# A GRU scan with an expert feed-forward beside it: first x copies ahead of the start state, sixteen early input shares, and GpSimd's weight splitting in smaller pieces over more steps

## What is computed

```python
def cell(h, x):                              # 32 steps, one after the other
    gi = x @ W_ih + b_ih                     # [32, 256] @ [256, 768]
    gh = h @ W_hh + b_hh
    r = sigmoid(i_r + h_r); z = sigmoid(i_z + h_z)
    n = tanh(i_n + r * h_n)
    return (1.0 - z) * n + z * h
# xt: the 1024 states
probs = softmax(xt @ w_router)               # 128 experts, top 4
basis = silu(xt @ w_gate) * (xt @ w_up)      # 8 bases of 128
out   = (mix of the bases by the 4 experts' coefficients) @ w_down
out  += (silu(xt @ shared_w_gate) * (xt @ shared_w_up)) @ shared_w_down
return x + out
```

## Time and profile before

| | us |
|---|---|
| median of 3 runs | 152.83 |
| lowest and highest | 152.21, 153.01 |
| the profiled execution | 153.46 |
| its span in the profile | 151.7 |

### The profile page before, as it was taken

The page is one execution under the profiler, slowest core; times in us unless marked ns, Lnnn a source line. Parts: engine busy times, 40 slices in busy tenths (PEclk is TensorE's granted clock), DMA queues, the critical chain, the costliest instruction groups (busy, mean ns, idle before and its releaser), DMA issues.

```text
span 151.7 us, 4005 instructions
## 1 busy us (share of the span) xinstructions
PE 137.6 (91%) x1480; PEld 97.8 (64%) x1480; DVE 110.7 (73%) x407; ACT 69.2 (46%) x224; POOL 63.6 (42%) x115
## 2 busy tenths in 40 slices
PE   7559798689798979999999999999999999899991
PEld 4236575457465557766776687667766777588881
DVE  2020868789979988898879777977797779858661
ACT  1200757865458246526633553256334542613730
POOL 1200515566315771474138314741465145657030
PEclk9955999999999999999999999999999999999999
DMA  2999980000000000010000000000010001000102
GB/s 79 312 371 210 288 278 5 4 4 0 0 0 4 0 0 4 2 35 6 0 16 23 0 0 12 29 0 6 2 36 0 0 4 37 0 0 0 35 4 69
DMA packets 5619, 7.12 MB, mean 47 GB/s; under 512 B 864, under 2 KB 4192, under 8 KB 5600
## 3 DMA queue, kind: packets, MB, share of 16 engines
q1 hardware_dynamic: 5180, 6.63, 15.2%
q10 hardware_dynamic: 420, 0.24, 0.6%
HBM read 5.81 MB, written 1.05 MB: 45 GB/s over the span
## 4 chain that ended last, share of the span: by engine, by line
PE 67%; DVE 19%; DMA 5%; ACT 4%; issue 2%; ACTq 1%; DVEq 0%
PE unit L609 29%; PE gates L600 14%; PE gates L561 8%; PE down L674 6%; DMA h<-in_cond_dram 5%; DVE sc_out L842 4%; DVE sc_add L836 2%; DVE keys L925 2%; PE unit L576 2%; DVE pre L833 2%; DVE hT L849 2%; ACT sc_add L416 2%; DVE m L830 1%; PE route L621 1%; PE route L655 1%
## 5 line engine op out<-in xcount | busy, mean ns | idle before, releaser
L306 POOL CAST hThi<-hT 128x64 fp32r<-128x64 f32 x32 | 8.2, 255 | 64.9 <-DVE hT L849 64.4
L609 PE MATMUL unit<-whi,hThi 128*128 128x512 f32 x80 | 33.8, 423 | 1.2 <-DVE shared L902 0.9
L409 ACT ACTIVATE trz<-gates 128x128 f32<-128x128 f32 x32 | 8.9, 277 | 53.2 <-PE gates L600 53.2
L600 PE MATMUL gates<-whh,hT 128*32 128x192 f32 x512 | 28.1, 338 | 4.6 <-DVE hT L849 4.5
L609 PE MATMUL unit<-whi,hTlo 128*128 128x512 f32 x80 | 31.6, 395 | 0.0
L609 PE MATMUL unit<-wlo,hThi 128*128 128x512 f32 x80 | 31.6, 395 | 0.0
L600 PEld LDWEIGHTS gates<-whh,hT 128*32 128x32 f32 x512 | 13.7, 111 | 16.1 <-DVE hT L849 8.7
L842 DVE TENSOR_TENSOR_SCAN sc_out<-sc_mul,sc_add 128x128 f32<-128x128 f32 x32 | 15.7, 492 | 7.2 <-ACT sc_add L416 7.0
L609 PEld LDWEIGHTS unit<-whi,hThi 128*128 128x128 f32 x80 | 15.1, 188 | 6.7 <-issue 2.7
L561 PE MATMUL gates<-wih,xT 128*32 128x192 f32 x320 | 17.8, 346 | 1.3 <-DVE xT L808 1.3
L609 PEld LDWEIGHTS unit<-whi,hTlo 128*128 128x128 f32 x80 | 15.0, 188 | 3.6
(11 more groups left out here) (126 smaller groups left out, 232.3 us busy)
## 6 DMA issues: line engine op xcount, KB each, us to landing
wraw<-in_L_ffn_w_gate_dram SPq DMA_DIRECT2D x2, 512.0 KB, 9.0
wraw<-in_L_ffn_w_up_dram SPq DMA_DIRECT2D x2, 512.0 KB, 11.2
out_dram<-ot SPq DMA_DIRECT2D x7, 128.0 KB
wih<-in_L_cond_W_ih_dram SPq DMA_DIRECT2D x1, 768.0 KB, 6.0
xtok<-in_x_dram SPq DMA_DIRECT2D x4, 192.0 KB, 9.3
whh<-in_L_cond_W_hh_dram SPq DMA_DIRECT2D x1, 512.0 KB, 7.2
whh<-in_L_cond_W_hh_dram SPq DMA_DIRECT2D x1, 256.0 KB, 6.1
wraw<-L_ffn_shared_w_gate_dram SPq DMA_DIRECT2D x1, 256.0 KB, 11.4
```

Source lines behind the costliest of these rows:

```text
L600: last = pe.matmul(g[Q * j:Q * (j + 1), HN:HN + 3 * FJ], st, whh[:, s, :].rearrange("p (g j c) -> p j g c", g=3, j=NJ)[:, j], start=False, ...
L609: last = pe.matmul(dst, st[:, p % 3, s, :, :].rearrange("p t b -> p (t b)"), w[:, s, :, cols], start=(s == 0 and n == 0), stop=(s == KB - ...
```

## The change

- **Start.** VectorE's two copies of the first x chunks stand ahead of its wait for the start state. W_ih comes in two transfers, one for each half of the contraction. TensorE's warming matmuls are 16, 0 and 3 in place of 13, 2 and 2. The rest of x is loaded ahead of the router's and the gate weights.
- **Early shares.** Sixteen steps in place of twelve have their input share made early, two of each chunk, all by step 5. All of x is transposed by step 3 instead of step 5; two of the three pairs are copied by VectorE instead of ScalarE.
- **Splitting.** The router's high part is made in step 1 instead of 0, its low part in step 2 instead of 0. The high parts stand in steps 2 to 6 instead of 0 to 6, the low parts in steps 3 to 8 instead of 0 to 6. GpSimd takes seven pieces instead of six, each as two instructions of 128x256; `lo_down` is three instructions of 128x256 and stands in step 10 instead of 9.

```diff
-WARM = 13
+WARM = 16
-EARLY = [4, 5, 6, 7, 8, 9, 12, 13, 10, 14, 16, 17]
-EARLY_PAIRS = [[0], [1], [2], [3], [4], [5]]
-TURN_PAIR = {1: 2, 3: 4, 5: 6}
-KEEP_PAIR = {1: 2, 3: 4, 5: 6}
-HI_AT = [(0, 1), (1, 2), (2, 4), (4, 5), (5, 7), (7, 9), (9, 10)]
-LO_VECTOR_AT = [[], [1], [3], [], [5], [7], []]
-LO_POOL_AT = [[0], [], [2], [4], [6], [8], [9]]
+EARLY = [4, 5, 6, 7, 10, 11, 14, 15, 18, 19, 22, 23, 26, 27, 30, 31]
+EARLY_PAIRS = [[0], [1], [2], [3, 4], [5], [6, 7]]
+TURN_PAIR = {1: 2, 2: 4, 3: 6}
+KEEP_PAIR_SCALAR = {1: 2}
+KEEP_PAIR_VECTOR = {2: 4, 3: 6}
+HI_AT = [(0, 0), (0, 0), (0, 2), (2, 4), (4, 6), (6, 8), (8, 10)]
+LO_VECTOR_AT = [[], [], [], [], [], [3], [5], [7]]
+LO_POOL_AT = [[], [], [], [0], [1], [2], [4], [6], [8, 9]]
...
             load_x(sp, range(0, 2), 0, 2, ld_xfirst)
-            sp.dma_start(wih[:, :, :], pairs(w_ih)).then_inc(ld_wih, 16)
+            for s in range(KB):
+                sp.dma_start(wih[:, s, :], pairs(w_ih)[:, s, :]).then_inc(ld_wih, 16)
...
+            load_x(sp, range(TC), 2, NC, ld_xrest)
             sp.dma_start(rraw[:, :, :], pairs(w_router)).then_inc(ld_router, 16)
...
-                if pair == 0:
-                    load_x(sp, range(TC), 2, NC, ld_xrest)
...
                 pool.wait_ge(w_hi, i + 2)
-                pool.tensor_tensor(wlo[:, s, :, cols], wraw[:, s, :, cols], whi[:, s, :, cols].bitcast(F32),
-                                   ALU.subtract).then_inc(w_lo_pool, 1)
+                for a in range(2):
+                    last = pool.tensor_tensor(wlo[:, s, a, cols], wraw[:, s, a, cols], whi[:, s, a, cols].bitcast(F32),
+                                              ALU.subtract)
+                last.then_inc(w_lo_pool, 1)
...
-                    if t == 2 * TC + 1:
+                    if t == TC + SKEW + 4:
                         lo_down()
...
-                if t == 0:
+                if t == 1:
                     hi_router()
...
-                        pe.wait_ge(x_pair_turned, 3)
+                        pe.wait_ge(x_turned, 4)
...
-            keep_warm(2)
             turn_x(0, route, 0)
             turn_x(1, unit_bank[2], 0)
-            keep_warm(2)
+            keep_warm(3)
...
+            keep_x(0)
+            keep_x(1)
             dve.wait_ge(ld_h0, 16)
             dve.transpose(hT0[:, :].rearrange("p (s b) -> p s b", s=KB), h0[:, :].rearrange("p (c s) -> p s c", s=KB)).then_inc(hT_ready, 1)
             dve.tensor_scalar(hhalf[:, :], h0[:, :], 0.5, None, ALU.mult).then_inc(hhalf_ready, 1)
-            keep_x(0)
-            keep_x(1)
...
+                if t in KEEP_PAIR_VECTOR:
+                    keep_x_pair(KEEP_PAIR_VECTOR[t])
-                if t == 0:
+                if t == 2:
                     lo_router()
```

More of the change, by code:

```diff
@@ L147, in build @@
         early_bank = unit_bank + [turned, down]
-        pair_bank = {2: route, 4: route, 6: route}
         scaled_up = qc[:, 0:2 * UW].rearrange("p (n c) -> p n c", n=2)
@@ L339, in lo_piece @@
                 pool.wait_ge(w_hi, i + 2)
-                pool.tensor_tensor(wlo[:, s, :, cols], wraw[:, s, :, cols], whi[:, s, :, cols].bitcast(F32),
-                                   ALU.subtract).then_inc(w_lo_pool, 1)
+                for a in range(2):
+                    last = pool.tensor_tensor(wlo[:, s, a, cols], wraw[:, s, a, cols], whi[:, s, a, cols].bitcast(F32),
+                                              ALU.subtract)
+                last.then_inc(w_lo_pool, 1)
             def lo_down():
                 pool.wait_ge(w_hi, len(PIECES) + 2)
-                pool.tensor_tensor(dlo_w[:, :, :], draw[:, :, :], dhi_w[:, :, :].bitcast(F32), ALU.subtract)\
-                    .then_inc(w_lo_pool, 1)
+                for a in range(3):
+                    last = pool.tensor_tensor(dlo_w[:, a, :], draw[:, a, :], dhi_w[:, a, :].bitcast(F32), ALU.subtract)
+                last.then_inc(w_lo_pool, 1)
             def mixing(f):
@@ L402, in keep_x_pair @@
                 act.wait_ge(x_raised, c + 2)
-                act.activation(xT[:, c:c + 2, :, :].rearrange("p c s n -> p (c s n)"), pair_bank[c][:, 0:4 * P],
-                               ACT.Copy)\
+                act.activation(xT[:, c:c + 2, :, :].rearrange("p c s n -> p (c s n)"), route[:, 0:4 * P], ACT.Copy)\
                     .then_inc(x_pair_turned, 1)
@@ L474, in prepare @@
                     load_gates(t + 2)
-                if t == 0:
+                if t == 1:
                     hi_router()
-                if t in KEEP_PAIR:
-                    keep_x_pair(KEEP_PAIR[t])
+                if t in KEEP_PAIR_SCALAR:
+                    keep_x_pair(KEEP_PAIR_SCALAR[t])
                 if t < len(HI_AT):
@@ L543, in wait_x @@
             def wait_x(t):
-                if t // TC < 2:
-                    pe.wait_ge(x_turned, t // TC + 1)
+                c = t // TC
+                if c < 2:
+                    pe.wait_ge(x_turned, c + 1)
+                elif c < 4:
+                    pe.wait_ge(x_pair_turned, 1)
                 else:
-                    pe.wait_ge(x_pair_turned, t // TC // 2)
+                    pe.wait_ge(x_turned, c // 2 + 1)
             def x_part(t):
@@ L557, in x_part @@
                 if t == 0:
-                    pe.wait_ge(ld_wih, 16)
+                    pe.wait_ge(ld_wih, 32)
                 for s in range(KB):
@@ L581, in turn_x_pair @@
             def turn_x_pair(c):
-                if c > 2:
-                    pe.wait_ge(x_pair_turned, c // 2 - 1)
-                else:
-                    pe.wait_ge(x_turned, 2)
-                turn_x(c, pair_bank[c], 0)
-                turn_x(c + 1, pair_bank[c], 1)
+                wait_x(TC * (c - 1))
+                turn_x(c, route, 0)
+                turn_x(c + 1, route, 1)
             def h_part(t):
@@ L809, in keep_x, with keep_x_pair @@
                     .then_inc(x_turned, 1)
+            def keep_x_pair(c):
+                dve.wait_ge(x_raised, c + 2)
+                dve.tensor_copy(xT[:, c:c + 2, :, :].rearrange("p c s n -> p (c s n)"), route[:, 0:4 * P])\
+                    .then_inc(x_turned, 1)
             def keep_early(n):
```

## The result

The changed kernel takes 152.65 us (median of 20 runs, 150.72 to 154.25) against 152.88 for the kernel before (20 runs, 151.71 to 153.59). The ratio to before is 0.9931, 95% interval 0.9905 to 0.9956.

What follows compares the result with a forecast made beforehand. Bounds: the start, then the recurrence's latency, then TensorE's work in the long stretch. Terms -1.95 + 4.05 - 0.25 - 3.6 = -1.75 us, from the profiled 153.46 to 151.7, hence a median of 151.0; range 148.4 to 153.4.

Steps and rivals of the forecast that it cites:

- H(1): Start of `h_part` (H) of step 1: predicted to move from 16.80 to 14.85 us, a gain of 1.95.
- x lands as before: Start: x's transfers stay first in both queues, so transposes still start at 7.81 us.
- Still early enough: Start: the last part of W_hh, with one more issue ahead, lands by 10.5 us at most, ahead of need.
- Step 8: Early steps: unit 3 waits for GpSimd's piece 6, with VectorE's piece 7 getting between; 4.5 us with the coefficients.
- Step 9: Early steps: unit 4 needs GpSimd's pieces 8 and 9, the latter there at 3.6 us; the step takes 4.4.
- the second half of the unit follows: Step 9: after GpSimd's piece 9, only half of unit 4 remains, 0.8 us.
- The long stretch: Steps 18 to 29: fewer just-in-time input shares, 14.4 us per four steps instead of 15.58; a gain of 3.6.
- Pieces covered: Rival, steps 8, 9 and 12: waits for GpSimd fall away, up to 2.65 us less, 148.4 us; chance 0.24.
- No earlier clock: Rival, start: TensorE's clock rises no earlier than before, costing 1.0 us, 152.0 us; chance 0.14.
- VectorE the bound: Rival, long stretch: VectorE falls behind TensorE; each 0.4 us per four steps costs 1.2, up to 153.4 or 154.6; chance 0.14.
- Halving turns against it: Rival, steps 6 to 11: VectorE gets in at ten new boundaries, delaying GpSimd's pieces; 3.3 us more, 154.3; chance 0.10.
- The wait for `em`: Near the end: TensorE's wait for VectorE grows from 0.35 to 1.0 us, using up step 30's 0.65; nothing gained.

Runs made afterwards that it cites:

- again: The changed kernel run once more, unchanged, for a second trace: median 152.43 us, ratio 0.9928 to the kernel before.
- spread_down11: Changed kernel with low-part pieces placed a step earlier, VectorE taking the last, and `lo_down` in step 11 instead of 10: 149.0 us, ratio 0.9753.
- d11_balance: `spread_down11` with VectorE's pieces 1, 3, 5, 7 in steps 3 to 6 and GpSimd's six in steps 2 to 7: 147.99 us, ratio 0.9657.
- warm9: Changed kernel plus twenty warming matmuls on TensorE in step 9, ahead of unit 4: 151.28 us, ratio 0.9884.
- d11_early12: `spread_down11` with the old twelve early shares, one pair in each of steps 0 to 5: 152.48 us, ratio 0.9969.
- spread_whole: Changed kernel with low-part pieces placed a step earlier, VectorE taking the last, and GpSimd's pieces as one instruction each: 150.88 us, ratio 0.9886.

## Why the prediction was right, and what it missed

The sum was made against the profiled execution, 151.7 us for its like. It took 151.24. That the profile fell into the lower heap is luck: the trace of `again`, with the same code, took 152.92. The forecast for the median, 151.0, missed the measured 152.65 mostly by what the sum did not have in it, the fall of the clock behind step 9. Term by term:

| term | predicted | measured in the profile |
|---|---|---|
| H(1) | 16.80 to 14.85: -1.95 | 14.57: -2.2 |
| steps 1 to 12 | 46.1: +4.05 | 45.9: +3.9 |
| steps 13 to 17 | 17.85: -0.25 | 17.8: -0.3 |
| steps 18 to 29 | 3 x 14.4: -3.6 | 3 x 14.35: -3.65 |
| from step 30 on | 0 | -0.05 |

**The start came out in sum, not by its steps.** "x lands as before" was wrong: it was used at 6.12, 1.7 earlier. "Still early enough" for W_hh was wrong: its last part was issued 0.5 later, as predicted, but landed 7.8 us after its issue and not 7.2, at 11.1, and with everything else earlier it is what opens step 0. The clock did not rise at 11.7; it had been at 1.0 since before 6 and fell there. That H(1) is so near is two errors against each other. A path much like the one that I described is that of other executions: `spread_down11` has the shares at 8.99 (predicted 9.5), H(0) at 11.55 (11.9) and H(1) at 15.00 (14.85).

**Steps 1 to 7** were 3.69, 3.41, 4.06, 2.92, 3.28, 3.62, 4.09 for 3.41, 3.41, 4.06, 2.95, 3.4, 3.7, 4.5. The first is longer by the clock, which is low until 15.1 (in `again`, with the clock back before H(1), it is 3.40). The last is 0.4 shorter than the sum had it, for a piece of 0.68 us ahead of the quarter k0; why was not traced.

**Step 8** was 4.42 for 4.5, and TensorE's wait named `wlo`, 0.78 us. But `spread_down11`, with no piece outstanding there, has the same 4.42: there TensorE waits 0.54 us for VectorE's `q`, and the coefficients close both steps 4.13 us after H(8). So GpSimd's piece had no price of its own; only `d11_balance`, where VectorE has no piece in step 7 either, gets 3.35. Right size, wrong wait.

**Step 9** was 4.89 for 4.4. The step that failed is "the second half of the unit follows": both waits stand ahead of the unit's first matmul, so unit 4 begins only when the second piece is there, at 47.39, and all six matmuls (48.95 - 47.39 = 1.6 us) come after it, not three. The piece itself was 0.3 earlier than in the sum (47.39 - 44.06 = 3.3 for 3.6). What I had not in the sum at all is the second cost of such a wait: in three of the four traces with a wait of 2.47 us TensorE ran at 1.2 GHz for some 3 us afterwards, a loss of 1.4 to 1.7 us over steps 9 to 12; by the times (11 of 20 in the upper heap) it may be about half of the executions. Filling the wait (`warm9`) brings the median from 152.65 to 151.28. I had looked for the clock at the start and not in the middle, though the terms of my sum had the wait in them.

**Step 12** was 4.23 for 4.25, with the wait for `mixed`; `spread_down11` confirms its cause.

**The long stretch.** 14.35 for 14.4, and `d11_early12` gives the 3.6 us back: the right term with the right cause. VectorE did not become the bound by more than the 0.1 of the forecast, and the tie was real:

```profile
80.89 0.25 DVE L855 STREAM_TRANSPOSE hT<-sc_out 128x64 f32<-128x64 f32 x1
81.14 0.41 DVE L921 TENSOR_REDUCE lx<-route 128x128 f32<-128x256 f32 x1
...
85.34 0.25 DVE L855 STREAM_TRANSPOSE hT<-sc_out 128x64 f32<-128x64 f32 x1
```

The state after the quarter k0 is there at 85.59, H(20) is 85.64 and 7.37 us after H(18) = 78.27, for 7.28 plus 0.1 as forecast. TensorE waits for it: step 19 takes 3.84 where the sum has 3.73 for its own work, and that is the 0.1.

**The rivals.** Pieces covered: no, TensorE waits 0.78 and 2.47 us for them, though the 0.78 costs nothing by itself. No earlier clock: in the profile the clock ran neither this way nor as forecast, as above. VectorE the bound: by 0.1 only. Halving turns against it: the reverse, whole pieces cost 1.6 us more in `spread_whole`, although a piece in halves takes GpSimd 1.41 to 1.43 us instead of 1.28. The wait for `em` grew by 0.07 only, from 0.35 to 0.42, not to 1.0. TensorE has a new wait of 0.29 us for VectorE's `shared` two microseconds ahead of it, and from H(31) to the transposed `em` it is 4.11 us (128.99 - 124.88) instead of 3.48, which uses up the 0.65 that step 30 gained. So the sum was right there (-0.05), the place of the wait was not.

**The working itself.** Some of its figures do not follow from its rows. The state after the quarter k0 is at 83.92 + 0.25 = 84.17, not 84.22. Three times 15.58 - 14.4 is 3.54, not 3.6. The halving makes nine new boundaries (seven pieces and two for the down weights), not ten, in steps 3 to 10; at 0.3 us each that is 2.7, not 3.3. And the floor for steps 8, 9 and 12 was set at 10.5 us with 3.4 for step 9, though the bare step is 2.92: the runs without these waits have 3.35, 2.92 and 3.54, together 9.81. None of this moves the forecast by over 0.1 us; the floor of the range would have been 0.7 lower.

## What to carry to other kernels

Take work that recurs in every turn of a long full stretch and put it where the engine waits anyway; that term was the easiest to size, and with the old list of shares the rest of the change was worth 0.3%. Spread a helper engine's pieces so that none is first started in the step that needs it, and remember that a wait of TensorE in the middle, like the one of 2.5 us here, can have a second price behind it in the clock, which shows in the spread of the times before it shows in any one trace. When transfers are reordered, look at each of them for who waits for it now, since one that was never late before, here W_hh, can become the next bound.
